# A 16-tap block convolution computed as three half filters over even and odd columns instead of four

## What is computed

```python
x = x + _L0_attn_a_ref(_layernorm(x), block_values, cols, rows)
...
xb = x.reshape(batch, n_block_row, bs, t)
x_unfold = xb[:, cols].reshape(batch, n_blocks * bs, t)
W = block_values.reshape(n_blocks * bs, bs, ks)
o = conv_general_dilated(x_unfold, W, window_strides=(1,), padding=[(ks - 1, 0)],
                         feature_group_count=n_blocks)
y = zeros((batch, n_block_row, bs, t)).at[:, rows].add(o)
```

## Time and profile before

| | |
|---|---|
| median of 3 runs | 873.48 us |
| lowest, highest run | 873.46, 874.2 us |
| span of the profiled execution | 873.0 us |
| that execution's time beside its span | not given apart from the three runs; the median is 0.5 us above the span |
| PE, DVE, ACT, POOL busy | 99%, 57%, 48%, 37% |
| granted TensorE clock | 1.00 throughout |
| moved by DMA | 61.0 MB, 38.0 MB of it before 160 us |

### The profile page before, as it was taken

The page is one execution under the profiler, slowest core; times in us unless marked ns, Lnnn a source line. Parts: engine busy times, 40 slices in busy tenths (PEclk is TensorE's granted clock), DMA queues, the critical chain, the costliest instruction groups (busy, mean ns, idle before and its releaser), DMA issues.

```text
span 873.0 us, 16737 instructions
## 1 busy us (share of the span) xinstructions
PE 865.5 (99%) x5617; PEld 773.3 (89%) x5620; DVE 501.8 (57%) x1360; ACT 420.0 (48%) x978; POOL 320.0 (37%) x293
## 2 busy tenths in 40 slices
PE   9999999999999999999999999999999999999998
PEld 7999878888888888889989998998997888888887
DVE  4777757333333338887688668768877433333334
ACT  3522416334334344776377557647746433434332
POOL 5211014556555564232121213212112556556552
PEclk9999999999999999999999999999999999999999
DMA  8999312111111102000000100000002111111111
GB/s 338 362 383 391 136 40 77 49 54 36 54 45 45 54 18 76 1 26 21 18 3 21 36 0 24 0 0 1 1 1 73 38 54 39 51 54 36 54 36 49
DMA packets 25554, 61.01 MB, mean 70 GB/s; under 512 B 3298, under 2 KB 10916, under 8 KB 25508
## 3 DMA queue, kind: packets, MB, share of 16 engines
q1 hardware_dynamic: 23204, 47.82, 16.1%
q0 software_dynamic: 2304, 12.58, 3.8%
HBM read 59.35 MB, written 1.05 MB: 69 GB/s over the span
## 4 chain that ended last, share of the span: by engine, by line
PE 93%; DVE 3%; ACT 1%; DMA 1%; issue 1%; POOL 0%; DVEq 0%; ACTq 0%
PE bank L1131 29%; PE bank L1655 25%; PE bank L1144 14%; PE bank L534 7%; PE bank L545 5%; PE bank L1781 4%; PE bank L1721 3%; PE bank L1157 2%; PE bank L1167 2%; DMA cv_shared<-in_wtaps 1%; PE bank L1746 1%; DVE cv_acc L421 1%; PE bank L518 1%; PE bank L1675 1%; PE bank L129 0%
## 5 line engine op out<-in xcount | busy, mean ns | idle before, releaser
L1030 DVE TENSOR_TENSOR f_h<-f_scaled,bank 128x512 f32<-128x512 f32 (+1 forms) x90 | 60.8, 676 | 179.4 <-POOL f_scaled L895 166.9
L812 ACT ACTIVATE f_h_hi<-f_h 128x512 fp32r<-128x512 f32 (+2 forms) x102 | 63.6, 624 | 186.2 <-DVE f_h L1030 186.0
L895 POOL TENSOR_TENSOR f_scaled<-f_act,f_gate_rows 128x512 f32<-128x512 f32 x80 | 102.9, 1287 | 116.3 <-ACT f_act L805 115.9
L1131 PE MATMUL bank<-f_xt_hi,f_w_lo 128*128 128x512 f32 x352 | 138.2, 393 | 0.0
L1131 PE MATMUL bank<-f_xt_hi,f_w_hi 128*128 128x512 f32 x352 | 137.8, 391 | 0.0
L1350 ACT ACTIVATE at_prob<-bank,at_sbias,at_qrs 128x512 f32<-128x512 f32 (+3 forms) x128 | 77.6, 618 | 72.6 <-DVE at_sbias L1542 72.6
L1037 DVE TENSOR_TENSOR f_h_lo<-f_h,f_h_hi 128x512 fp32r<-128x512 f32 (+2 forms) x102 | 71.8, 704 | 70.7 <-ACT f_h_hi L812 70.4
L1131 PE MATMUL bank<-f_xt_lo,f_w_hi 128*128 128x512 f32 x352 | 108.8, 390 | 0.0
L1144 PE MATMUL bank<-f_w_lo,f_h_hi 128*128 128x256 f32 (+1 forms) x352 | 99.6, 283 | 0.0
L1144 PE MATMUL bank<-f_w_hi,f_h_lo 128*128 128x256 f32 (+1 forms) x352 | 99.6, 283 | 0.0
L1144 PE MATMUL bank<-f_w_hi,f_h_hi 128*128 128x256 f32 (+1 forms) x352 | 99.3, 282 | 0.0
(11 more groups left out here) (232 smaller groups left out, 2062.8 us busy)
## 6 DMA issues: line engine op xcount, KB each, us to landing
cv_raw<-in_wconv SPq DMA_DIRECT2D x26, 512.0 KB, 6.7
cv_shared<-in_wtaps POOLq DMA_DIRECT2D x16, 768.0 KB, 7.7
f_wraw<-in_w SPq DMA_DIRECT2D x42, 256.0 KB, 2.6
xn<-in_wconv SPq DMA_DIRECT2D x14, 512.0 KB, 6.5
f_wraw<-in_w SPq DMA_DIRECT2D x42, 128.0 KB, 2.5
at_wraw<-in_wqkv SPq DMA_DIRECT2D x3, 768.0 KB, 4.4
at_oraw<-in_wo SPq DMA_DIRECT2D x4, 512.0 KB, 3.5
X<-in_x_tiles SPq DMA_DIRECT2D x2, 512.0 KB, 8.0
```

The source lines that it names most:

```text
L812: a.activation(h_hi[slot][0:rows, cols], h_f[half][0:rows, cols], ACT.Copy).then_inc(s["h_hi_done"], 1)
L895: g.tensor_tensor(scaled[half][:], act[half][:], gate_rows[:, half * HALF:(half + 1) * HALF], ALU.mult).then_inc(s["scaled_done"], 1)
L1030: v.tensor_tensor(h_f[half][0:rows, cols], src[half][0:rows, cols], pu[half][0:rows, cols], ALU.mult)\
L1131: mm = t.matmul((pg, pu)[gu][half][0:out_rows, :], w, x, start=q == 0, stop=q == 3 * KH - 1)
```

## The change

Columns are split into even ones, x0, and odd ones, x1, and taps likewise into h0 and h1. Instead of the four products of half filters, three are computed: (h0 + h1) with x0, which goes into both output phases; h1 with XA = x1 one column earlier minus x0; and h0 with XB = x1 minus x0. Each half filter has 8 taps, that is 4 steps of two, so there are twelve subfilters: f = 0 to 7 (h by parity of f) and `FIR` + 0 to 3 for the summed taps. Each product has 2 x 128 moving columns. The host reorders the taps (`TAPS`).

- **Input.** VectorE writes x0 and x1 apart (lower channels), GpSimd makes XA and XB (`differences`) and copies the upper channels to `xp` in 8 operations (`upper_rows`), which stand ahead of tap chunk 1 on its queue. TensorE waits for them ahead of step 0's products. Rounding and splitting of the input take 64x768 elements instead of 64x1024 each.
- **Weights.** GpSimd adds pairs of steps: `pair_sums` (16 times 128x128), `low_pair` (twice 128x1024), `added_pair_sums` (four times 128x512, behind the last block). ScalarE copies all 512 columns of a bank to `full`. There are ten rounding pieces instead of six (`ADDED_ORDER`).
- **PSUM.** Bank 3 now collects the common product, so sums have three banks.
- **Order.** Blocks behind the low parts are 4, 5 and 5 to 6 per bank instead of 5, 5 and 6, with 42 instead of 34 in the last step. Step 0's products stand behind step 1's sums. The last pieces follow `LAST_PRODUCTS`.
- **End.** The common product is added to both phases by a broadcast (`add_common`); both batches of the last row are added behind one end.

```diff
-        BANKS = 4
+        BANKS = 3
+        P2_BANK = 3
...
-        LAST_ORDER = (2, 3, 0, 1)
-        APART = 3
+        FIR = NST
+        ADDED_ORDER = ((5, 0), (7, 0), (FIR + 2, 0), (5, 1), (FIR + 2, 1), (7, 1), (FIR + 3, 0), (6, 0), (FIR + 3, 1), (6, 1))
+        LAST_PRODUCTS = ((5, 0), (FIR + 2, 0), (FIR + 2, 1), (FIR + 3, 0), (FIR + 3, 1), (6, 0), (7, 0), (5, 1), (6, 1), (7, 1))
...
-        BANK_BLOCKS = ((5,) * 8, (5,) * 8, (6, 6, 6, 6, 6, 4, 0, 0))
-        PACE = (0, 0, 2, 2, 4, 4, 6, 8)
-        LAST_PACE = (0, 0, 2, 2, 4, 4, 4, 8)
+        BANK_BLOCKS = ((4,) * 8, (5,) * 8, (6, 6, 5, 5, 5, 5, 5, 5))
...
-                    a.activation(full[slot][:, :, cols], sums[:, NLOW:NW, :], ACT.Copy)
+                    a.activation(full[slot][:, :, cols], sums, ACT.Copy)
...
+            def differences(b):
+                x = xs[b]
+                g.wait_ge(s["xn_ready"], GC * b + LG)
+                g.tensor_tensor(x[:, :, XB, :], x[:, :, X1, :], x[:, :, X0, :], ALU.subtract).then_inc(s["x_parts"], 1)
+                g.tensor_tensor(x[:, :, XA, 1:M], x[:, :, X1, 0:M - 1], x[:, :, X0, 1:M], ALU.subtract).then_inc(s["x_parts"], 1)
+                g.tensor_tensor(x[:, :, XA, 0:1], xp[:, 0:LG, b, 0:1], x[:, :, X0, 0:1], ALU.subtract).then_inc(s["x_parts"], 1)
+            def upper_rows(b):
...
+                        g.tensor_copy(xp[k * BS:(k + 1) * BS, par::2, b, lo:lo + D], xh[b][par * BS:(par + 1) * BS, :, :])\
...
+            def pair_sums(i, q):
...
+                g.tensor_tensor(full[1][:, 0:NLOW, cols], full[1][:, 0:NLOW, cols], full[0][:, 0:NLOW, cols], ALU.add)\
+            def added_pair_sums(i, r):
+                other = full[0][:, 0:NLOW, :] if i == 2 else acc[:, 1, 0:NLOW, :]
+                g.tensor_tensor(row_part(low_of(FIR + i), r), row_part(acc[:, 0 if i == 2 else 2, 0:NLOW, :], r),
+                                row_part(other, r), ALU.add).then_inc(s["pair_sums"], 1)
...
-                bank = ps[APART][:, 0:D] if apart else ps[4 + r][:, batch.start * D:batch.stop * D]
-                hi, lo = (x[:, c, batch, bass.ds(tap, D)] for x in (xc_hi, xc_lo))
+                if f >= FIR:
+                    stream, tap, bank = X0, 2 * (f - FIR), ps[P2_BANK][:, r * D:(r + 1) * D]
+                else:
+                    h = 1 - f % 2
+                    stream, tap, bank = (XA, XB)[h], 2 * (f // 2), ps[4 + r][:, h * D:(h + 1) * D]
+                hi, lo = (x[:, c, :, stream, tap:tap + M] for x in (xc_hi, xc_lo))
...
+            t.wait_ge(s["x_parts"], 3 * B + 4 * B)
+            for u in units(0):
+                products(*u)
```

More of the change, by code:

```diff
@@ L30 @@
 XPITCH = 272
+M = D // 2
+FT = KS // 2
+SPITCH = 136
+TAPS = [(1 - st % 2) + 4 * (st // 2) + 2 * k for st in range(NST) for k in range(2)]
 NPE, ND = 5, 3
@@ L180, in conv_phase @@
                          .rearrange("p (w o) -> p w o", w=NLOW) for i in range(2)] for part in range(2))
-        ws_hi += [sb(f"ws_hi{i}", [P, NLOW, BS], F32R)[:] for i in range(2, ND + 1)]
-        ws_lo += [sb(f"ws_lo{i}", [P, NLOW, BS], F32R)[:] for i in range(2, ND + 1)]
-        full = [sb(f"full{i}", [P, NW - NLOW, BS], F32) for i in range(2)]
+        ws_hi += [sb("ws_hi2", [P, NLOW, BS], F32R)[:]]
+        ws_lo += [sb("ws_lo2", [P, NLOW, BS], F32R)[:]]
+        for part, w in enumerate((ws_hi, ws_lo)):
+            w += [late[:, (2 * i + part) * CHUNK:(2 * i + part + 1) * CHUNK].rearrange("p (w o) -> p w o", w=NLOW)
+                  for i in range(2)]
+        full = [sb(f"full{i}", [P, NW, BS], F32) for i in range(2)]
         acc = sb("acc", [P, ND, NW, BS], F32)
@@ new lines, in gpsimd @@
+            powers(1)
+            differences(1)
+            clear_sums(range(3, ZEROED))
+            g.wait_ge(s["rstd_ready"], B)
+            tap_blocks(0)
+            for b in range(B):
+                upper_rows(b)
+            g.wait_ge(s["x_parts"], 7 * B)
+            for q in range(4):
+                pair_sums(0, q)
+            tap_blocks(1)
+            for q in range(4, 6):
+                pair_sums(0, q)
+            tap_blocks(2)
+            for q in range(6, SB):
+                pair_sums(0, q)
@@ new lines, in gpsimd @@
+            d = 3
+            for st in range(2, NPE):
+                for q in range(SB):
+                    if st == 3:
+                        pair_sums(1, q)
+                    while d < NDC and DB * (d - 2) <= blocks_behind(st, q):
+                        tap_blocks(d)
+                        d += 1
+                    if st % 2 == 0 and q == 1:
+                        low_pair(st // 2 - 1)
+            g.wait_ge(s["ws_hi_done"], NPE * SB)
+            g.wait_ge(s["pair_lo_done"], 2)
@@ L349, in gpsimd @@
+            g.wait_ge(s["added"], 2 + 2 * NBLK)
+            for i in (2, 3):
+                for r in range(LG):
+                    added_pair_sums(i, r)
             first_weights["low"](g)
@@ L609, in sum_and_convolve, with units, paced @@
                         t.wait_ge(s["ws_lo_done"], st * SB)
-                    for c, r in LOW_PAIRS[n:pace[q]]:
-                        products(st - 1, c, r)
-                    n = pace[q]
-                finish_products(st - 1)
+                    for f, c, r in woven[q]:
+                        if f >= FIR:
+                            t.wait_ge(s["pair_lo_done"], f - FIR + 1)
+                        products(f, c, r)
+            def units(f, part=slice(0, len(LOW_PAIRS))):
+                return [(f, c, r) for c, r in LOW_PAIRS[part]]
+            def paced(f):
+                return [units(f, slice(lo, hi)) for lo, hi in ((0, 0), (0, 0), (0, 2), (2, 2), (2, 4), (4, 4), (4, 6), (6, 8))]
             t.wait_ge(s["onehot_ready"], 1)
```

296 lines of the change are left out of this document (169 added, 127 removed).

## The result

The changed kernel takes **914.39 us** (median of 4 runs, 914.15 to 915.21), the kernel before 873.76 beside it: a ratio of 1.0466, 95% interval 1.0451 to 1.0481. The forecast was 868.9 us and a range up to 875.5. The forecast has the wrong sign, and the loss (40.6 us) is nine times the gain that it named (4.55).

A forecast was written before the change was run, and what follows sets the result against it. TensorE, busy 99%, was taken as the bound, with VectorE and DMA close behind. The convolution's end 5.85 us earlier and 1.3 us back at the hand-over made -4.55: 868.9 us, range 862 to 875.5.

The forecast's parts named there:

- TensorE's own work: Convolution products: 192 matmuls at 0.233 us become 288 at 0.116, 44.8 to 33.4 us, 11.4 us less.
- Rival (d): Products: the 256-column matmul with two runs takes 150 ns, not 116, ten pieces 4 us more, 873 us; chance 0.02.
- the estimate of 98 ns from the issue gap: Products: the skill page's pace, interpolated to 256 columns; products would go from 25.2 to 28.2 us, costing 3 us.
- granted in full: TensorE's clock in the first two stretches of the convolution, up to 101.6 us, as read from the trace before.
- so waits little: Start of step 2: TensorE has three banks to go on with until 44.7, bank (2,0)'s low part coming at 44.0.
- rival (b): Start: GpSimd's chain is longer, copies of 1.29 us plus waits, last block at 106.8, time 876 us; chance 0.17.
- the point of no gain: GpSimd's copies at the start: from about 1.26 us each, waits included, the 4.55 us gain is used up (with +20.7).
- VectorE's term: Middle stretch to the last block: 49.5 us of VectorE's work plus 7.1 us for GpSimd's operations holding it.
- rival (c): Late taps: VectorE's wait for them comes on top, last block at 104.5, time 872 us; chance 0.15.
- Behind the last block: From last block added to end of products: +19 us, where it was 24.55 before; end at 120.3 instead of 126.15.
- the worst case of the prediction: Behind the last block: low parts strictly alternate with GpSimd's added sums, products end at +20.7 us.
- The hand-over: Last product to last scaling: 4.3 us instead of 3.0, both batches added behind one end, 1.3 us back.

The follow-up runs named there:

- 1: The changed kernel without its six conditional TensorE bodies (products of pairs that don't occur) and so without the jumps: 891.6 us (1.0201).
- 6: The changed kernel with every jumped body cut to 48 matmuls (512 columns moved at once) and three jumps at the end instead of one of 240: 892.9 us (1.0214).
- 2: The kernel before with the jumped bodies of steps 0 to 4 lengthened from 48 to 80 matmuls, no executed instruction changed: 896.4 us (1.0264).
- 11: The kernel before with five of its jumped bodies of 64 matmuls in place of 48: 884.13 us (1.0126).
- 12: The kernel of 8 with step 4's blocks dealt 5, 5, 5, 5, 5, 5, 6, 6, and the last four pair sums on VectorE instead of GpSimd: 875.99 us (1.002).
- 13: The kernel of 12 with the three last jumps at pieces 0, 2 and 4, so 24 matmuls between them instead of 12: 873.15 us (0.999).
- 7: The kernel of 6 with GpSimd's upper-row copies made only if the flag asks, so tap chunk 1 goes out right behind chunk 0: 879.67 us (1.0049).
- 10: The kernel of 8 with step 4's larger banks dealt last and two blocks moved from step 3 to step 4: 877.78 us (1.0044).
- 14: The kernel of 12 without jumped bodies and jumps, products of pairs that don't occur left out of the program: 871.74 us (0.998).
- 8: The kernel of 7 with GpSimd's low part of a pair made in four quarters: 876.76 us (1.0032).
- 5: The changed kernel with TensorE's convolution written twice, the version with all products jumped over once at the start: 912.38 us (1.0435).
- 3: The kernel before with TensorE waiting for three extra ScalarE copies behind step 0's products: 882.15 us, median of ten (1.0087).
- 4: The kernel before with TensorE waiting for one extra ScalarE copy behind step 0's products: 874.91 us (1.001).

## Why the prediction was wrong

**TensorE's own work: right.** Triples of 256 columns start 0.35 us apart after the change:
```profile
37.34 0.40 PE L669 MATMUL bank<-cv_xc_hi,held 128*128 128x256 f32 x2
...
37.69 0.40 PE L669 MATMUL bank<-cv_xc_hi,held 128*128 128x256 f32 x2
```
as in the earlier trace rows, two runs of elements or not: 117 ns a matmul. Rival (d) (150 ns) and the estimate of 98 ns from the issue gap don't agree with it.

**The step that failed** is a term that the working put at nothing: the branches, whose bodies grew from 48 matmuls to 80 and from three times 48 to one of 240 in the same diff and don't run; and with it the clock, "granted in full" before by the earlier trace rows and taken to stay so. The runs put 22.8 us on them (after against 1), nearly all through their length (6), and 2 and 11 show the same in the kernel before, at 22 and 10 us. The other 17.3 us are the second step that failed, "so waits little": waits for VectorE were priced in idle time alone (rival (b) below). Half filters also make short jumps costly, since the same number of instructions lasts half as long: with 12 matmuls between the jumps over 48, TensorE has no gap where they take 2.8 us (before), and gaps of 1.0 to 1.9 us where they take 1.4 (12); with 24, 2.8 us, one of 0.47 is left (13). That it makes the long bodies of 80 worse as well is not shown: they cost 22 us in 2.
The Trainium skill, page "Runtime: NRT & Kernel Launch", section "Instruction fetch mechanics", says it in a line that the prediction did not weigh: "Branching breaks sequential prefetch", a taken branch whose target lies outside the two pages that are held waits for a fetch. The traces agree, by the landings named above, and so does it that not every jump of one length stalls (those at 72.3 and 136.2 us did not). The page gives no price, and it has the crossing of a page "mostly hidden", which a jump often is not: 0.3 to 6.6 us here.

**Rival (b), GpSimd's chain is longer: right in direction, not in price.** The copies took 1.05 us each (0.9 forecast with waits; the point of no gain was 1.26). Chunk 1 was issued at 38.2 instead of 34.8: 2.3 of these 3.4 us had come up before the first copy (28.0 instead of 25.7), 1.2 in the copies. The low part of (2,0) came at 47.05 (44.0). The rival's sign, TensorE idle from 36 to 39, did not show: it waited 0.19 us for the copies, at 36.4. Its bill was 876 us, 2.5 above before; taking the copies out brought 13 us (6 against 7, by medians that spread over 9 and 14 us), because a wait for that low part can take the clock with it.

**VectorE's term: sized well.** GpSimd's 2.38 us cost eight adds 3.75 - 1.44 = 2.31, forecast 2.26. From 44 us to the last block the adds took 273 ns each instead of 251, 5 us on 240, for which 7.1 were set. The last block came at 136.9 after the change, at 115.7 without branches, at 104.9 with full clock (10) and at 103.4 in 14, against 101.3. Some of what remains is rival (c)'s, late taps: in 8 VectorE waited for them 1.15 us at 85.8. How much, no run separates.

**Behind the last block: mis-sized.** +20.9 without branches (115.7 to 136.56), the worst case of the prediction (+20.7) and not +19. Low parts alternate with GpSimd at 1.76 us, as the earlier trace rows would have it; without GpSimd's sums (14) it is 103.4 to 120.61, +17.2.

**The hand-over: mis-sized.** Set at 4.3 us from the last product to the last scaling; in 14 the scaling ends at 126.36, 5.7 us behind it (before: 3.0); there the first half's add stands behind a 1.28 us low part of the next stage on VectorE. That is 1.4 us more than was set. About another microsecond went to half clock there: the 512-column products of the next stage start 0.43 us apart from 127.8 to 129.0 instead of 0.23.

With all that mended the half filters bring 5.5 us at the end of the convolution (forecast 5.85), and 1.7 in the profiled span or 2.4 by the medians, against the 4.55 of the forecast. So its mechanism exists, at a third to a half of its size, and only in a program without the jumps, with the copies gone and the sums moved. With the jumps the best is 13, which can't be told from the kernel before. That 5.5 comes so close to 5.85 is partly luck: the last block is 2.1 us later than forecast, and the work behind it 1.8 us shorter, since 14 makes the sums on VectorE.

## What to carry to other kernels

Code that is only jumped over has a price: count the instructions in every body that a branch skips, before and after, above all when the instructions around it get shorter; keep the body short, and leave work between jumps. When TensorE is the bound, a wait of a microsecond is not a microsecond: look for what the clock did behind it, since a half clock stands as full busy time. And a gap at the first instruction behind a branch that is put down to a semaphore should be held against the time at which that semaphore's work really ended, as 13 shows, and against the instruction transfers.

## What was not expected of the hardware

- The clock of TensorE stayed at 1.2 GHz for long although TensorE was busy throughout: 3.4 us in 13 (93.4 to 96.8), 41 us after the change (43.2 to 84.2), 56 us in 5 (16.8 to 73.3).
- Whether a wait brings the fall is not fixed by its length: with a pause of 1.76 us put in, seven of ten executions had a mean clock below 1 (3), with 0.72 us none of ten (0.999 or 1.000, as before; 4). The wait of 0.57 us at 47.2 in the profiled execution of 7 was followed by half clock from 49.7, that of 1.88 us at 101.0 in 10 was not. What decides it stays open; no run here separates it.
- In the kernel before the gap behind a jump grew with the length skipped (1.35 us at 64, 3.3 and 3.6 at 80); after the change it was 1.4 to 3.6 at 80, 4.7 at 240 and 6.6 over a whole convolution (5). It also grew with less work since the last jump (12 against 13). A jump stalls where the transfer of its instructions lands too late; why it starts when it does was not tried.
